# One elementwise product moved from GpSimd to VectorE, and two box sums moved with it

## The reference, cut to what matters

```python
t1 = p1_w * x                                  # p1_w: one factor a channel and a row
t2 = x + t1
t4 = relu(x)
t5 = unfold(x, 3, 7)                           # 21 shifted copies of every channel
t7 = einsum('oc,nchw->nohw', p7_w, t4)
t12 = mean over 5 taps of (x - shifted t7)
t10 = grouped 1x1 convolution of t2 with p10_w # 4 groups, 128*21 outputs
t11 = einsum('nck,nmk->ncm', t1, t5) / 64
t13 = einsum('ncm,nmk->nck', t11, t10) / sqrt(128*21)
out = maximum(t13, t12)
```

## Time and profile before

| what | value |
| --- | --- |
| median of the runs (lowest, highest) | 423.63 us (423.4, 424.42) |
| the profiled execution: its own time | 423.14 us |
| its span in the trace | 421.3 us |
| TensorE busy | 402.2 us, 95% of the span |
| VectorE busy | 336.1 us, 80% |
| ScalarE busy | 252.5 us, 60% |
| GpSimd busy | 93.7 us, 22% |
| mean granted TensorE clock | 0.982 of full speed |
| chain of waits that ended last | 86% TensorE, 6% VectorE |

### The profile page before, as it was taken

How to read it: one execution, slowest core, us unless ns; L and a number is a source line. 1 busy time by engine, 2 the same in 40 slices (tenths; PEclk the granted TensorE clock), 3 DMA queues, 4 the chain that set the end, 5 groups by cost and what they waited for, 6 DMA issues and landing times.

```text
span 421.3 us, 12375 instructions
## 1 busy us (share of the span) xinstructions
PE 402.2 (95%) x5126; PEld 243.5 (58%) x5126; DVE 336.1 (80%) x397; ACT 252.5 (60%) x721; POOL 93.7 (22%) x78
## 2 busy tenths in 40 slices
PE   6699599999999999999999999999999999999995
PEld 2134366544854557444766667444587878665563
DVE  8669987888888888888868888888878888686804
ACT  2226481777547771777637773577717776377970
POOL 3504520133003320033203320033200331033300
PEclk9789699999999999999999999999999999999999
DMA  8941335545476635744465634655356443533105
GB/s 317 404 197 59 108 98 199 180 166 166 139 216 194 227 109 174 267 169 159 160 203 183 213 105 150 229 212 201 129 188 225 159 159 101 203 127 100 53 27 201
DMA packets 24104, 72.40 MB, mean 172 GB/s; under 512 B 2800, under 2 KB 3056, under 8 KB 24048
## 3 DMA queue, kind: packets, MB, share of 16 engines
q1 hardware_dynamic: 24048, 71.61, 49.5%
HBM read 54.82 MB, written 16.78 MB: 170 GB/s over the span
## 4 chain that ended last, share of the span: by engine, by line
PE 86%; DVE 6%; issue 3%; POOL 2%; DMA 1%; ACT 1%; DVEq 0%; SPq 0%; ACTq 0%
PE ps_y L571 47%; PE ps_y L583 15%; PE ps_p L583 12%; PE ps_t L583 12%; DVE yT L432 1%; DMA u_planes<-w_tiles 1%; DVE ps_y L421 1%; DVE pair_sum L442 1%; POOL u_sum L213 1%; DVE v_planes L413 1%; POOL u_planes L219 1%; POOL u_planes L216 0%; DVE v_planes L411 0%; DVE v_planes L403 0%; ACT q_sb L241 0%
## 5 line engine op out<-in xcount | busy, mean ns | idle before, releaser
L571 PE MATMUL ps_y<-v_planes,u_planes 64*64 64x512 f32 x2048 | 261.4, 598 | 5.1 <-DVE ps_y L423 4.0
L571 PEld LDWEIGHTS ps_y<-v_planes,u_planes 64*64 64x64 f32 x2048 | 122.1, 135 | 105.5 <-issue 70.6
L207 POOL TENSOR_TENSOR t1T<-t1T,p1T_sb 128x512 f32<-128x512 f32 x64 | 84.4, 1346 | 295.6 <-DVE box L450 198.7
L583 PE MATMUL ps_p<-box,p_fifth 64*64 64x512 f32 x480 | 128.0, 597 | 4.2 <-DVE box L459 4.2
L302 ACT ACTIVATE t<-xn,p_plus 128x64 f32<-128x64 f32 x512 | 128.2, 335 | 0.0
L583 PE MATMUL ps_t<-t,aT 64*64 64x512 f32 x448 | 118.1, 589 | 0.0
L241 ACT ACTIVATE base<-ps_p 128x512 f32<-128x512 f32 x60 | 35.8, 597 | 92.2 <-PE ps_p L583 92.2
L583 PEld LDWEIGHTS ps_y<-t1T,yT 64*64 64x64 f32 x2048 | 58.0, 133 | 9.1 <-DVE yT L432 5.1
L583 PE MATMUL ps_y<-t1T,yT 64*64 64x128 f32 x2048 | 60.7, 270 | 2.5 <-issue 1.7
L421 DVE TENSOR_TENSOR ps_y<-ps_y,q_sb 128x512 f32<-128x512 f32 x32 | 22.4, 699 | 45.1 <-ACT q_sb L241 45.1
L583 PEld LDWEIGHTS ps_p<-box,p_fifth 64*64 64x64 f32 x480 | 39.3, 134 | 27.4 <-issue 15.5
(11 more groups left out here) (39 smaller groups left out, 106.7 us busy)
## 6 DMA issues: line engine op xcount, KB each, us to landing
xw<-x_conv SPq DMA_DIRECT2D x32, 594.0 KB, 5.2
xn<-x_nat SPq DMA_DIRECT2D x32, 512.0 KB, 4.1
t1T<-x_pix SPq DMA_DIRECT2D x32, 512.0 KB, 6.3
out<-base SPq DMA_DIRECT2D x64, 256.0 KB, 2.4
u_planes<-w_tiles SPq DMA_DIRECT2D x4, 384.0 KB, 5.8
p1T_sb<-p1T SPq DMA_DIRECT2D x1, 128.0 KB, 6.4
p_sb<-p7T SPq DMA_DIRECT2D x1, 64.0 KB, 6.0
p_sb<-p SPq DMA_DIRECT2D x1, 32.0 KB, 6.2
```

The source lines that it names most:

```text
L207: nc.gpsimd.tensor_tensor(part, part, p1T_sb[:, e, :].unsqueeze(1).broadcast_to([P, 4, C]), ALU.mult).then_inc(t1_ready, 1)
L571: last = nc.tensor.matmul(dst[TILE * pair:TILE * pair + TILE, :], u_planes[rows, u % GROUPS, weights, TILE * k:TILE * k + TILE], v_planes[ ...
L583: last = nc.tensor.matmul(dst[cols, 0:data.shape[-1]], weights[rows, cols], data[rows, :], start=start, stop=False, skip_group_check=True)
```

## The change

GpSimd's eight products an image are gone. VectorE makes the same product in four instructions of 128 by 1024 elements, `t1_quarter(n, q)`: the first in slot C of image n, two in slot D, the last in slot A of the next image. `box_pairs(n, 1)` and `box_fours(n, 1)` move from slot C to slot B, ahead of `seeds(4n+1)`, and `box_last(n, 1)` from slot D to slot C. On ScalarE `relu(n, 1)` moves ahead of the eight instructions of `t2_half(n-1, 5)`, but for the first image. TensorE waits for four counts of `t1_ready` an image in place of eight.

```diff
 gpsimd
-            for n in range(N_IMG):
-                pool.wait_ge(box_steps, BOX_STEPS * (4 * n + 1) + 2)
-                for q in range(3):
-                    t1_part(n, q)
-                pool.wait_ge(box_steps, BOX_STEPS * (4 * n + 2) + 1)
-                for q in range(3, 6):
-                    t1_part(n, q)
-                pool.wait_ge(box_steps, BOX_STEPS * (4 * n + 2) + 3)
-                for q in range(6, 8):
-                    t1_part(n, q)
 scalar
                 seed_x(n - 1, 6)
                 copy_two(u + 1)
+                if n > 0:
+                    relu(n, 1)
                 t2_half(n - 1, 5)
 
-                relu(n, 1)
+                if n == 0:
+                    relu(n, 1)
                 base_half(n - 1, 6)
 vector
+            def t1_quarter(n, q):
+                e, j = q // 2, 8 * (q % 2)
+                dve.wait_ge(xp_loaded[q], 16 * (n + 1))
+                part = t1T[:, e, j:j + 8, :]
+                nc.vector.tensor_tensor(part, part, p1T_sb[:, e, :].unsqueeze(1).broadcast_to([P, 8, C]),
+                                        ALU.mult).then_inc(t1_ready, 1)
...
             box_sums(0, 0)
+            dve.wait_ge(small_loaded, SMALL)
+            t1_quarter(0, 0)
             turn_y(0)
...
             box_fours(0, 1)
+            t1_quarter(0, 1)
             turn_y(1)
...
             box_pairs(0, 2)
+            t1_quarter(0, 2)
             for n in range(1, N_IMG):
...
                 box_last(n - 1, 2)
+                t1_quarter(n - 1, 3)
                 max_half(n - 2, 6)
                 seeds(u)
...
                 second_part_of_a(n - 1)
                 box_sums(n, 0)
                 max_half(n - 1, 0)
+                box_pairs(n, 1)
+                box_fours(n, 1)
                 seeds(u + 1)
 
                 turn_y(u)
                 planes_low(u + 3)
                 max_half(n - 1, 1)
                 planes_high(u + 3)
-                box_pairs(n, 1)
-                box_fours(n, 1)
+                box_last(n, 1)
+                t1_quarter(n, 0)
                 max_half(n - 1, 2)
                 seeds(u + 2)
 
                 turn_y(u + 1)
                 planes_low(u + 4)
                 max_half(n - 1, 3)
                 planes_high(u + 4)
-                box_last(n, 1)
                 box_pairs(n, 2)
+                t1_quarter(n, 1)
+                t1_quarter(n, 2)
                 max_half(n - 1, 4)
                 seeds(u + 3)
             turn_y(UNITS - 2)
+            t1_quarter(LAST, 3)
             max_half(LAST - 1, 5)
 tensor
-                    pe.wait_ge(t1_ready, 8 * n + 8)
+                    pe.wait_ge(t1_ready, 4 * n + 4)
```

More of the change, by code:

```diff
@@ L202, in _ @@
         def _(pool):
[L203 to L208, removed]
             def weights(g):
```

## The result

| | before | after |
| --- | --- | --- |
| median of 4 runs each, us | 424.02 | 439.0 |
| lowest and highest | 423.4, 424.95 | 437.69, 440.85 |
| ratio, with its 95% interval | | 1.0354 (1.031 to 1.0399) |
| the profiled execution, own time and span | 423.14, 421.3 | 440.85, 439.0 |

A forecast was written before the change was run, and what follows sets the result against it. TensorE was taken as the bound, busy 48.76 of 49 us an image. Span 421.3 + 16.8 (stops) - 0.25 (tail) = 437.9 us, 439.7 with the 1.84 us around it, the median put at 440; range 430 to 447 us.

The forecast's parts named there:

- The bound, and the product's price: Steady images: TensorE is the bound, busy 48.76 of 49 us; each product on VectorE costs 1.14 us.
- Slots A and D: VectorE's idle time ahead of seeds there covers the added products, with 0.3 us left; cost nothing.
- The wait for the relu: Slot B: box_pairs(n, 1) waits some 2.4 us for ScalarE's relu, making VectorE 3.45 us late.
- The two stops: TensorE, images 1 to 7: waits for seeds, then for max_half, 2.40 us an image, +16.8 us in all.
- The first part: Slot C: TensorE's zero_three waits for the late seeds(4n+1), stopping 1.27 us.
- the second stop: t13_rows(n-1, 2) waits for max_half(n-1, 1) to free its bank, about 1.1 us, bringing TensorE's lateness to 2.40 us.
- rival (2): Only TensorE's wait for seeds counts, 7 times 1.27 is 8.9 us, so 432 us; chance 0.07.
- The head: Before image 1: two products come in, two delays beside GpSimd go; zero, 2 us either way for the clock.
- The tail: Last product's 0.41 us wait for yT shrinks as contention with GpSimd goes: -0.25 us, at most -0.4.
- Rival (3): TensorE's clock falls at the stops: some 452 us if every second image, 463 if each; chance 0.10.
- The sum: Whole kernel: 421.3 + 16.8 - 0.25 = 437.9 us of span, forecast 440 us.

The follow-up runs named there:

- Experiment 1: The changed kernel with relu(n, 1) on ScalarE moved ahead of base_half(n-1, 5): 423.07 us beside 423.12 for the kernel before, ratio 0.9992.
- experiment 2: The kernel before, products left on GpSimd, only the two box sums, box_last and the relu moved as in the change: 440.68 us, ratio 1.0414.
- experiment 3: The changed kernel with max_half(n-1, 1) moved ahead of turn_y and planes_low on VectorE: 432.14 us, ratio 1.0228.
- experiment 6: Experiment 1 with GpSimd multiplying quarters 0 and 1 of image 0 as they land, and box_last(0, 1) right behind box_fours(0, 1): 421.22 us, ratio 0.9958.
- experiment 8: Images 1 to 7 as in Experiment 5, the head as in experiment 6: 420.79 us beside 423.31 for the kernel before, ratio 0.994.
- experiment 4: The changed kernel with box_pairs, box_fours and box_last of quarter 1 moved back, products still on VectorE: 424.94 us, ratio 1.0049.
- Experiment 5: experiment 4 with VectorE's products spread, one in each slot: 422.03 us beside 423.05 for the kernel before, ratio 0.9974.

## Why the prediction was right

**The bound, and the product's price.** As predicted: TensorE's slots outside the stops keep 10.30 us, and a product takes 1.13 us from start to start (238.97 to 240.10), 1.219 of its own. Slots A and D hold theirs: 0.3 us were predicted to be left in each, 0.34 and 0.37 are.

**The wait for the relu.** Predicted 2.4 us of idle time, measured 2.32 in image 4 and 15.8 in seven. The signal from ScalarE to VectorE that I had put at 0.11 us was 0.03. VectorE's delay was predicted as 3.45 us and is 3.38. Experiment 1 shows the cause, since it takes away this wait and nothing else; experiment 2 shows that it is enough.

**The two stops.** Predicted 2.40 us an image in all, measured 12.77 - 10.30 = 2.47. The first part was predicted as 1.27 us. Counted from the copy of q, `zero_three` began 223.26 - 218.91 = 4.35 us after it and now 233.59 - 228.04 = 5.55: 1.20. The rest, 1.27 us, is the second stop's, where 1.13 was predicted: I had TensorE start 0.05 us after `max_half`, and it starts 0.14 after. Seven times 2.47 is 17.3 us, where I had 16.8. That the second stop counts, against rival (2), is shown by experiment 3, which takes it away: 0.95 us an image less by the intervals, and a ratio of 1.0228 against 1.0354, with intervals that don't overlap.

**The head.** Predicted: nothing, with 2 us either way for the clock. VectorE and TensorE in the head (L396 is `planes_high`, L444 `box_last(0, 1)`):

```profile
41.21 0.75 DVE L396 TENSOR_TENSOR v_planes<-xw 128x576 f32<-128x576 f32 x1
...
43.88 1.22 DVE L444 TENSOR_TENSOR box<-box,relu_pad 128x1024 f32<-128x1024 f32 x1
```

```profile
45.15 0.91 PE L584 MATMUL ps_p<-box,p_fifth 64*64 64x512 f32 x2 [3.09 <-DVE box L444]
...
58.04 4.16 PE L584 MATMUL ps_y<-t1T,yT 64*64 64x128 f32 x144 [0.39 <-DVE yT L417]
```

The delays beside GpSimd did go, as reckoned: `planes_high` is back at 0.75 us from 1.83. The Trainium skill's rule that was weighed there (page SBUF — State Buffer, section Who interferes with whom) agrees with these rows, and experiment 2 adds one from the steady part: GpSimd's instructions then lie beside `planes_high`, and it takes 1.22 us in image 4.

`box_last(0, 1)` comes at 43.88 instead of 45.13, and the first product at 58.04 instead of 59.74, 1.7 us earlier. None of that is shown to be the change's. 1.26 us of it is there at the first `seeds(1)`, ahead of any product (23.75 against 25.01): between 16 and 24 us the mean granted clock is 0.79 in this trace and 0.57 in that of the kernel before, which is some 3.4 us at 1.2 GHz against 6.8. From `seeds(1)` to `box_last(0, 1)` it is 20.13 us now and was 20.12, just as reckoned. The last 0.45 us lie behind the stop: from its end to the first product it is 58.04 - 45.15 = 12.89 us, and was 59.74 - 46.40 = 13.34. There the clock is 0.79 between 44 and 52 us, and was 0.58. Experiment 2, whose program is that of the kernel before up to this point, has a clock of 0.79 there too, and the same 12.89 us:

```profile
46.69 0.65 PE L586 MATMUL ps_p<-box,p_fifth 64*64 64x512 f32 x2 [4.21 <-DVE box L462]
...
59.58 2.63 PE L586 MATMUL ps_y<-t1T,yT 64*64 64x128 f32 x88 [0.39 <-DVE yT L435]
```

So the head's term was right at zero, and the 1.7 us are luck of the two traces.

**The tail.** Predicted -0.25 us, since the wait for yT before the last product goes. That wait is gone. From the last copy of q to the last product it is 10.78 us (404.62 to 415.40), and was 11.06 (386.53 to 397.59): -0.28. From the last copy to the end it is 34.38 against 34.77, -0.39; the other 0.11 us lie behind the last A.

**The clock.** Rival (3) had TensorE's clock fall at the stops. It doesn't: in the seven stretches of 51 us that I took between 57 and 415 us the clock is 1.00 in all but one. Stretches of one image, in the columns of the earlier trace rows, images 3 and 4:

```profile
160.00:211.00 51.00, 49.78 (x652) 31.31 (x648) 45.12 (x54) 31.25 (x90) 0.00 (x0) 1.00 0.53 173
211.00:262.00 51.00, 47.68 (x597) 31.44 (x592) 41.46 (x49) 27.94 (x81) 0.00 (x0) 0.97 0.49 165
```

The one fall, in image 4, comes behind another kind of stop, in the product, which nobody released by a semaphore:

```profile
218.59 1.37 PE L584 MATMUL ps_y<-t1T,yT 64*64 64x128 f32 x34 [2.13 <-issue]
219.56 1.07 PE L572 MATMUL ps_y<-v_planes,u_planes 64*64 64x512 f32 x2
```

2.13 us of "issue", then matmuls at half speed (1.07 us where 0.60 is usual) for some 3 us: 3% of the 51 us are lost. By the oscillation that the Trainium skill describes (page TensorE: Matmul & The Clock Gate, section on the second HAM failure mode), the fourteen short stops of images 1 to 7 should have cost clock as well; none of those rows shows it, so that rival falls for stops of this length (0.83 and 0.35 us of idle time in the records). It came nearer than that sounds: the stop of 1.75 us in the heads of experiments 6 and 8 is followed by a clock of 0.50.

**The sum.** 421.3 + 17.3 for the stops - 1.7 in the head - 0.4 behind the last copy of q is 436.5 us. The remaining 2.5 of the span of 439.0 lie in the seven products: the intervals between the copies of q that hold them sum to 126.67 us against 124.18. Image 4's alone is 3.4 us longer, 1.9 from its stop (2.13 us, and 0.24 before) and the rest from the clock behind it.

Of all this the change's own part is 17.3 - 0.4 = 16.9 us. The medians differ by 15.0, and the interval of the ratio is 13.1 to 16.9 us, so the slots' sum lies at its edge. The median was predicted as 440.0 and is 439.0 us; with four runs that spread over 3 us, that the two agree within 1 us is in part luck. What bears the prediction out is the slots, which repeat to 0.01 us.

## What to carry to other kernels

Idle time in front of a wait isn't free space for just any work: what is put there has inputs of its own, and they may come from the very engine that the wait is for. Here the moved instruction needed a relu that stood behind the copy whose arrival had made the gap. So look up, for each instruction moved forward, where its inputs stand in their engine's list, and then follow the lateness past the first wait that it hits: the second one behind it, for a bank with a single buffer, doubled the price. What experiments 3 and 4 still lose is a wait for that bank as well. Experiment 5 shows the other half: a product whose inputs are there fits into the same idle time.

## What the runs showed of the hardware that was not expected

TensorE stops by itself in the product of y and t1, with "issue" as the releaser, in every kernel of the study, from 0.15 to 2.13 us. Its places are fixed in the program: behind the stop 34 records of the product are left in image 4, 49 in image 5 and 59 in image 6, in the changed kernel and in experiment 2 alike, and wherever another kernel stops in one of these images it is at the same record. The length changes from trace to trace. The longest was followed by a clock of 0.50; the next, 1.22 us in experiment 2, wasn't. What TensorE waits for there no run was made to show.

TensorE's clock stood at 1.2 GHz for some 3 us in some traces and for some 7 in others, with the same program up to there: ahead of its first rise (the changed kernel 3.4 us, experiment 5 6.8), and behind the stop in the head (experiment 8 3.4 us, experiment 6 6.8, both after an idle time of 1.75 us). Each such step moves the end by some 0.5 to 2 us. Together with the stops in the product that is enough to make up the 3 us over which runs of one kernel spread, though no two runs of the same kernel were compared for it.
